# Loading both expert numbers of a pair on DVE ahead of the activation product

## The reference

```
x = x + L0_ffn(L0_cond(x))        # diffusion step, then mixture of experts
x = x + L1_ffn(L1_cond(x))        # masked attention pooling, then fp8-rounded product

# L0_ffn, with E = 8 experts, K = 2 chosen, H = I = 256
logits = x @ router_weight ; top 2 ; scores = softmax(top 2)
gu   = x @ gate_up_proj[e] + gate_up_proj_bias[e]
gate = min(gu[..., ::2], 7) ; up = clip(gu[..., 1::2], -7, 7)
act  = (up + 1) * gate * sigmoid(1.702 * gate)
out  = sum over chosen e of score * (act @ down_proj[e] + down_proj_bias[e])
```

## Time and profile before

| | |
|---|---|
| median of 3 runs | 450.09 us (449.05 to 450.28) |
| the profiled execution | 451.54 us, span 449.8 us |
| PE, DVE, ACT, POOL busy | 81%, 76%, 47%, 38% of the span |
| experts' stage | about 105 to 310 us |
| granted PE clock from 106 to 310 us | 1.00 |

### The profile page before, as it was taken

The page is one execution under the profiler, slowest core; times in us unless marked ns, Lnnn a source line. Parts: engine busy times, 40 slices in busy tenths (PEclk is TensorE's granted clock), DMA queues, the critical chain, the costliest instruction groups (busy, mean ns, idle before and its releaser), DMA issues. The chain is left out here.

```text
span 449.8 us, 8322 instructions
## 1 busy us (share of the span) xinstructions
PE 366.1 (81%) x2222; PEld 303.9 (68%) x2222; DVE 342.5 (76%) x845; ACT 211.7 (47%) x364; POOL 169.8 (38%) x186
## 2 busy tenths in 40 slices
PE   0969787758899899999999999994398947987872
PEld 0858676746777788788888888883245536886761
DVE  5688899967777887788877877873799465778882
ACT  3725444312434344444434444342356456799971
POOL 5026777777734433245433333335100032031121
PEclk9969899658999999999999999999589959799975
DMA  6996622256644333233332322110998100036355
GB/s 197 369 315 208 248 102 90 98 172 205 200 140 122 98 97 94 80 108 102 97 97 85 105 87 91 44 49 16 382 355 301 39 0 0 1 48 93 49 78 109
DMA packets 41325, 58.13 MB, mean 129 GB/s; under 512 B 6462, under 2 KB 30914, under 8 KB 41154
## 3 DMA queue, kind: packets, MB, share of 16 engines
q1 hardware_dynamic: 31106, 36.62, 25.7%
q0 software_dynamic: 10176, 20.98, 15.8%
HBM read 31.15 MB, written 27.34 MB: 130 GB/s over the span
## 5 line engine op out<-in xcount | busy, mean ns | idle before, releaser
L594 POOL DMA_INDIRECT y_rows<-outs,slot_dst x71 | 72.4, 1019 | 117.5 <-ACT outs L688 104.7
L574 POOL DMA_INDIRECT regions<-flow,slots x64 | 69.1, 1080 | 42.9 <-DVE slots L1260 25.1
L910 PE MATMUL gu_banks<-gu_hi,rowT_hi 128*128 x142 | 60.0, 422 | 1.9 <-DVE rowT_lo L1330 1.9
L910 PE MATMUL gu_banks<-gu_hi,rowT_lo 128*128 x142 | 56.6, 399 | 0.0
L910 PE MATMUL gu_banks<-gu_lo,rowT_hi 128*128 x142 | 56.6, 398 | 0.0
L1342 DVE TENSOR_TENSOR gu_sum<-gu_banks,gu_bias 128x512 f32<-128x512 f32 x71 | 48.7, 687 | 9.3 <-issue 5.3
L1330 DVE TENSOR_TENSOR rowT_lo<-bank,rowT_hi 128x512 fp32r<-128x512 f32 (+1 forms) x37 | 24.8, 670 | 30.8 <-ACT rowT_hi L670 30.8
L675 ACT ACTIVATE gelu<-gu_sum 128x512 f32<-128x512 f32 (+1 forms) x37 | 22.8, 615 | 50.8 <-DVE gu_sum L1350 49.7
L680 ACT ACTIVATE actT_hi<-bank 128x512 fp32r<-128x512 f32 (+1 forms) x37 | 21.5, 581 | 42.7 <-PE bank L940 42.7
L910 PE MATMUL bank<-dn_hi,actT_hi 128*128 x142 | 41.1, 289 | 0.0
L910 PE MATMUL bank<-dn_hi,actT_lo 128*128 x142 | 40.0, 282 | 0.0
(11 more groups left out here) (313 smaller groups left out, 962.8 us busy)
## 6 DMA issues: line engine op xcount, KB each, us to landing
rows<-regions SPq DMA_DIRECT2D x71, 136.0 KB, 2.1
picks<-y_rows SPq DMA_DIRECT2D x16, 512.0 KB, 7.2
X<-in_x SPq DMA_DIRECT2D x8, 512.0 KB, 8.4
gu_lo<-in_L_ffn_gate_up_proj SPq DMA_DIRECT2D x8, 512.0 KB, 7.9
out<-X SPq DMA_DIRECT2D x7, 512.0 KB, 7.0
out<-ffn_sum POOLq DMA_DIRECT2D x7, 512.0 KB, 5.6
dn_lo<-in_L_ffn_down_proj SPq DMA_DIRECT2D x8, 256.0 KB, 8.7
gu_bias<-_L_ffn_gate_up_proj_bias SPq DMA_DIRECT2D x1, 2048.0 KB, 10.2
```

The costliest lines, as they stand in the source:

```text
L574: pool.indirect_dma_start(out=regions, out_offset=bass.IndirectOffsetOnAxis(ap=slots[:, n, c, t:t + 1], axis=0), in_=flow[:, n % FS, t, :] ...
L594: pool.indirect_dma_start(out=y_rows, out_offset=bass.IndirectOffsetOnAxis(ap=slot_dst[:, m:m + 1], axis=0), in_=outs[:, m % UNROLL, :], i ...
L910: mm = pe.matmul(acc, left[:, cols], right[:, ds(expert), part, :].rearrange("p e f -> p (e f)"), start=(not begun and part == 0 and left ...
```

## The change

`biased` no longer loads the number itself. A new function `numbers_of(g)` loads the numbers of both blocks of step g, and the loop calls it after `rows_low(g + 1)` and ahead of `activated(g - 1)`; `biased` takes the register from a table. Nothing else changes, on DVE or on another engine: DVE has 985 instructions before and after.

```diff
+            numbers = {}
+
+            def numbers_of(g):
+                for n in steps[g]:
+                    numbers[n] = dve.value_load(block_expert[0:1, n:n + 1], min_val=0, max_val=E - 1)
+
             def biased(g, i):
                 n = steps[g][i]
-                expert = dve.value_load(block_expert[0:1, n:n + 1], min_val=0, max_val=E - 1)
+                expert = numbers.pop(n)
                 dve.wait_ge(gu_psum, n + 1)
...
                 if g + 1 < STEPS:
                     rows_low(g + 1)
+                if g < STEPS:
+                    numbers_of(g)
                 if 0 <= g - 1 < STEPS:
                     activated(g - 1)
                 if g < STEPS:
                     biased(g, 0)
```

## The result

The changed kernel takes **460.0 us** (median of 6 runs, 457.1 to 461.4) against 449.9 us (6 runs, 448.9 to 451.3) beside it: a ratio of 1.021, 95% interval 1.018 to 1.024. It is slower by 10.1 us. The prediction had 456.2 in a range of 452.0 to 460.5. So the sign holds, the time lies at the upper edge of the range, and the loss is 1.6 times the +6.2 of the sum. The profiled execution took 458.65 us with a span of 456.9.

The account below looks back on a forecast made before the run. The prediction took a ring through three engines, with PE's own 5.35 us per plain pair just above it, as the bound. Terms +3.0, +0.5, +3.1, -1.6 and +1.2 gave +6.2 us, forecast 456.2 us, range 452.0 to 460.5.

Parts of the forecast that it names:

- the ring: Expert-stage dependency cycle through three engines, one rowT_lo to the next: 5.13 us alone, 5.62 after the change.
- slack of 0.22: Between activation product and PE's turn in plain pairs: the product can slip 0.22 us for free, and not more.
- rival A: No slack before PE's turn, so every 0.49 us of product delay is seen: 459 us; chance 0.22.
- B: Loads are free, sent by DVE while rowT_lo waits: 443 us; chance 0.06.
- C: Loads overlap and fit, product slips less than about 0.33 us: change wins, 446 us at 0.19; chance 0.05.
- (a): 11 plain pair periods of the experts: 5.62 us against 5.35, +0.27 each, +3.0 us together.
- (b): The one expert period of 5.14 us, which has no slack: +0.5 us.
- (c): 8 periods with a wide side job between the bias additions, its load already hidden: +3.1 us together.
- (d): 12 periods with chains of small jobs and an exposed second load: the change gains, -1.6 us together.
- (e): First pair's bias additions 0.4 us later, last three steps' product about 0.33 late: +1.2 us together.
- slow loads at the start of the stage: Upper bound: early loads stay at 0.55 to 0.78 us against 0.30, five pairs pay another 1.5 us: 460.5.

Follow-up runs that it names:

- small instructions: Both loads behind the product, plus 4 or 8 tiny DVE operations ahead of slot_dst: 0.9887 or 1.0142 of the time before the change.

## Why the prediction was right in sign and short in size

**What bounds the kernel.** The ring was the right unit, and its slack of 0.22 holds (small instructions). PE's 49.3 busy us of 50 were no bound in the sense that other losses vanish behind them. Over two plain pairs PE was busy 10.69 of 10.69 us before (265.04 to 275.73) and 11.15 of 11.50 after (264.97 to 276.47), for the same work, so its busy time isn't the time that its work needs. The plain periods of 5.81 to 5.83 look like the prediction's sign of rival A (5.8); the small instructions show that they are not.

**What a load costs, and when it starts.** 0.60 each, strictly one after the other, begun with rowT_lo: product at 1.36 to 1.39, predicted 1.35, but for two early pairs with slow loads (1.63 and 1.49). DVE's issue idle in front of it came to 15.3 us in 35 places, predicted about 16 in 34. Rivals B and C had no part. The rule of the Trainium skill behind B ("Perfetto Trace Analysis", section "Per-engine timelines"), that the sequencer is ready for the next instruction while a DVE instruction waits in its queue, doesn't carry over to register loads: in every record read here the loads behind a waiting instruction start only once it is released (106.0 behind 105.94, 270.8 behind 270.80).

**The terms.** The sum over all periods of the stage, in us:

| term | predicted | measured | with POOL's stores later |
|---|---|---|---|
| (a) 11 plain periods | +3.0 | +4.1 | +3.3 |
| (b) the one without slack | +0.5 | +0.9 | +1.7 |
| (c) 8 with a wide side job | +3.1 | +4.0 | +3.2 |
| (d) 12 with narrow chains | -1.6 | -0.5 | -2.5 |
| (e) first and last steps | +1.2 | +1.4 | +0.9 |
| sum | +6.2 | +9.9 | +6.6 |

Every term is off in the same direction, which suggests one cause and not a wrong sign or a missing place. The last column, the changed kernel with the later stores against the kernel before, brings (a) and (c) to the forecast. (b) is a period at the start of the stage, and differed between executions (+0.9 here, +0.6 when the changed kernel ran again); it and (d) miss in opposite directions, so that the last sum comes so near to +6.2 is luck in part.

**The step that failed** is one that the terms (a), (c) and (d) share: the prediction took the durations of DVE's instructions over from the trace of before, while it moved them by half a microsecond against POOL. So each of the terms (a), (c) and (d) came out too low, the three together by 3.1 us. The rows show what this did. First a plain pair of the changed kernel; the store that goes with the clipping at 269.03 (0.59), and gelu and the next store behind it:

```profile
268.38 0.98 POOL L594 DMA_INDIRECT y_rows<-outs,slot_dst  x1 [0.30 <-issue]
...
269.65 0.63 ACT L675 ACTIVATE gelu<-gu_sum 128x512 f32<-128x512 f32 x1 [1.26 <-DVE gu_sum L1356]
```

```profile
274.04 0.98 POOL L594 DMA_INDIRECT y_rows<-outs,slot_dst  x1 [0.30 <-issue]
...
275.32 0.63 ACT L675 ACTIVATE gelu<-gu_sum 128x512 f32<-128x512 f32 x1 [1.09 <-DVE gu_sum L1356]
```

The store ends at 269.36, and the clipping that began 0.65 into it ends at 269.62, 0.26 behind it; gelu starts 0.62 after the clipping's start. In the next pair the clipping begins 0.83 into the store, which is nearly over, takes its usual 0.42, and gelu starts 0.45 after it. In the kernel before, the first clipping began 0.35 into the store and wasn't held:

```profile
268.44 0.98 POOL L594 DMA_INDIRECT y_rows<-outs,slot_dst  x1 [0.30 <-issue]
```

```profile
268.79 0.42 DVE L1350 TENSOR_SCALAR gu_sum<-gu_sum 128x512 f32<-128x512 f32 x1
269.12 0.55 DVE L1351 TENSOR_SCALAR up<-gu_sum 128x512 f32<-128x512 f32 x1
```

The second one was (0.55 instead of 0.42), but ACT doesn't need it for gelu, and its product comes much later. The change moved the hold from an instruction with cover to the one that gates the ring. (Before and after, the pair with the wide job:)

```profile
190.02 0.98 POOL L594 DMA_INDIRECT y_rows<-outs,slot_dst  x1 [3.77 <-ACT outs L688]
...
190.04 0.48 DVE L1399 TENSOR_SCALAR k_scaled<-k_raw,scales 128x512 f32<-128x512 bf16 x1
```

```profile
188.48 0.69 DVE L1330 TENSOR_TENSOR rowT_lo<-bank,rowT_hi 128x512 fp32r<-128x512 f32 x1 [0.85 <-ACT rowT_hi L670]
...
190.51 0.98 POOL L594 DMA_INDIRECT y_rows<-outs,slot_dst  x1 [3.90 <-ACT outs L688]
191.08 0.67 DVE L1405 TENSOR_SCALAR k_scaled<-k_raw,scales 128x512 f32<-128x512 bf16 x1
...
194.45 0.69 DVE L1330 TENSOR_TENSOR rowT_lo<-bank,rowT_hi 128x512 fp32r<-128x512 f32 x1 [0.85 <-ACT rowT_hi L670]
```

The job started with the store and took 0.48; now it starts 0.57 into it and takes 0.67, ending 0.26 behind the store. The period is 5.97 where the prediction had 5.70 to 5.76 for such pairs. The narrow chains, which were to pay for it all:

```profile
176.31 0.69 DVE L1330 TENSOR_TENSOR rowT_lo<-bank,rowT_hi 128x512 fp32r<-128x512 f32 x1 [0.85 <-ACT rowT_hi L670]
...
178.34 0.98 POOL L594 DMA_INDIRECT y_rows<-outs,slot_dst  x1 [3.94 <-ACT outs L688]
178.91 0.41 DVE L1397 TENSOR_SCALAR kind_row<-kind_row 1x8 f32<-1x8 f32 x1
...
179.49 0.69 DVE L1348 TENSOR_TENSOR gu_sum<-gu_banks,gu_bias 128x512 f32<-128x512 f32 x1
...
182.29 0.69 DVE L1330 TENSOR_TENSOR rowT_lo<-bank,rowT_hi 128x512 fp32r<-128x512 f32 x1 [0.85 <-ACT rowT_hi L670]
```

As predicted, no issue idle is left in front of the second bias addition. But an instruction on eight numbers takes 0.41 instead of 0.18, until the store is over (179.32), and the period is 5.98 where 5.80 was predicted and 5.91 stood before. The gain of 0.11 was eaten.

The Trainium skill has the rule that was overlooked: "SBUF — State Buffer", section "SBUF: two separate sides", says that DVE in a two-port mode and GpSimd arbitrate for one pair of ports, that whichever starts first holds it for the whole instruction, and that the other fully blocks. That these DVE instructions run in such a mode is not shown by any run here. The rows agree with the blocking: each held instruction ends at the store's end or 0.26 behind it. They don't agree with a lock over the store's whole span: in the kernel before, the first clipping ran inside it at full speed.

**How much of the gap is that?** The gap is 3.7 us in the profiles. Moving POOL away gave back 3.1 in the medians, with plain pairs at 5.66, wide ones at 5.68 to 5.80 (the two with jobs of 0.68 at 5.98 and 5.99, where the prediction had 5.97) and the narrow ones from 170 us on at 5.71 to 5.97. The rest may be a product offset 0.03 over the forecast in 30 periods, about 0.9 at most; a test of that alone was not run.

**What was luck.** The time of 460.0 lies inside the range, but the upper end of 460.5 was set by rival A and by slow loads at the start of the stage. A is false, and slow loads made two products later by 0.25 and 0.11. What filled that room was for the most part POOL's hold, which the prediction doesn't name. (Its own terms add up to 456.3 and B and C to 0.11, where it has 456.2 and 0.10; nothing hangs on that.)

## What to carry to other kernels

A register load is hidden where the engine still has queued work behind the last released wait, up to the sum of that work (here 1.5 us, two loads); so it belongs behind the instruction that another engine waits for. Between a wait and that instruction it is free only as far as other queued work covers it: here one load was, two were not. Slack of a ring is small and must be measured against the next link: here 0.22 us, beyond which 0.63 more of delay cost 0.63. And when an edit shifts instructions in time, look at what POOL does at their new place: durations read from the old trace hold only for the old overlap.

## What the hardware showed that was not expected

- One-input DVE instructions on SBUF (clippings, scale, narrow ones) that begin 0.57 to 0.65 us into POOL's 0.98 us indirect store are stretched until its end: 0.42 to 0.59, 0.48 to 0.67, about 0.2 to 0.41. Those that begin 0.02 or 0.35 into it keep their duration. The thirteen kept traces together place the border: of 160 clippings of 128x512 that begin 0.51 to 0.79 into a store, 156 end 0.23 to 0.28 behind it, and of 151 that begin up to 0.50 into one, 140 take 0.44 or less. Why the first part of the store doesn't hold them was not tried.
- The hold can make a steady state of period two (5.83 and 5.67). From one pair to the next the store moves by 5.66 (268.38 to 274.04) and the clipping by 5.84 (269.03 to 274.87), so that the next clipping comes 0.83 into the store and escapes. The earlier plain pairs of the same kernel show that it need not: there each clipping is held a little, and every period is 5.73 or 5.74.
- DVE's sequencer loads registers while instructions sent before still wait for the engine (the load at 286.6 with two clippings queued), though in no record read here did it pass one that waited for a semaphore. Of the loads of the kernel with both ahead of rowT_lo 18 took over 0.35 us instead of 0.30 (the second of the pair shown 0.50), and 17 of them lie beside an indirect DMA of POOL; others beside one took 0.30 to 0.31, and what makes the difference was not tried.
- Both numbers behind the product make this kernel about 1.4% faster than it was before, by an edit of one place from the one that made it 2.1% slower.
